# Long-convolution filters read as ready-made Toeplitz blocks instead of being reversed on TensorE

## The reference, cut to what matters

```python
# v = layernorm(x), x1 = x2 = ctx, 8 channels per head, 32 heads h, L = 512
kv = vr[:, :, :, None, :] * x2r[:, :, None, :, :]
y  = irfft(rfft(kv, n=2*L) * rfft(k, n=2*L), n=2*L)[..., :L]   # causal convolution with filter k[h]
y  = y + kv * skip
out = einsum('bhijl,bhil->bhjl', y, x1r)
```

## Time and profile before

| | before |
|---|---|
| median of 3 runs | 3232.25 us (3229.4 to 3232.57) |
| the profiled execution: its time | 3230.03 us |
| its span, first to last instruction | 3228.3 us |
| mean granted TensorE clock | 0.992 of full |
| busy: PE, PEld, DVE, ACT, POOL | 97%, 83%, 67%, 39%, 35% |
| the loop over heads | about 24 to 640 us of the span |
| DMA | 285.83 MB, 89 GB/s in the mean |

### The profile page before, as it was taken

One profiled execution on the slowest core, in us unless ns is written; L12 is line 12 of the kernel. 1 busy time (PEld: TensorE's weight loads), 2 busy tenths in 40 slices (PEclk: granted clock), 3 DMA queues, 4 the chain that ended last, 5 costly groups with the idle time before them and its releaser, 6 DMA issues.

```text
span 3228.3 us, 50126 instructions
## 1 busy us (share of the span) xinstructions
PE 3135.5 (97%) x18517; PEld 2679.9 (83%) x18517; DVE 2167.3 (67%) x5741; ACT 1256.3 (39%) x3041; POOL 1120.6 (35%) x1176
## 2 busy tenths in 40 slices
PE   7999999999999779999999999999999999999999
PEld 4666666689899669999999999999999788888887
DVE  6888888755555568888888888888878533333332
ACT  2333333333344345555555555555555311111111
POOL 7877777625344322222222222222201111011110
PEclk9999999999999899999999999999999999999999
DMA  4544443259777731111111111111100300000000
GB/s 128 153 141 143 132 130 102 77 177 334 226 230 227 246 104 53 47 39 41 47 47 40 41 47 47 47 47 47 47 27 27 108 33 27 27 27 26 27 14 14
DMA packets 129409, 285.83 MB, mean 89 GB/s; under 512 B 18840, under 2 KB 19488, under 8 KB 129168
## 3 DMA queue, kind: packets, MB, share of 16 engines
q1 hardware_dynamic: 100080, 186.49, 18.7%
q0 software_dynamic: 29088, 96.13, 9.1%
HBM read 177.98 MB, written 104.58 MB: 88 GB/s over the span
## 4 chain that ended last, share of the span: by engine, by line
PE 79%; DVE 10%; POOL 7%; DMA 2%; ACT 1%; issue 1%; SPq 0%; POOLq 0%; DVEq 0%
PE g_PH L2444 4%; PE t_U L1727 4%; PE g_O L2460 4%; PE g_PH L2446 4%; PE g_O L2458 4%; PE g_O L2459 4%; PE g_PH L2445 4%; PE t_U L1728 4%; POOL c_kf L1308 4%; PE t_U L1729 4%; PE t_T L1703 3%; DVE c_R L1030 2%; PE t_PO L1713 2%; PE t_PO L1714 2%; DVE c_z L1024 2%; PE t_PO L1715 2%
## 5 line engine op out<-in xcount | busy, mean ns | idle before, releaser
L1857 ACT ACTIVATE t_pr<-t_sm,t_nb 128x256 f32<-128x256 f32 x512 | 256.7, 502 | 368.5 <-DVE t_nb L2067 368.5
L2238 POOL TENSOR_TENSOR t_r<-t_r 128x256 f32<-128x256 f32 x128 | 94.3, 736 | 771.0 <-DVE t_r L2046 425.1
L2516 DVE CAST g_hh<-g_hf 128x512 fp32r<-128x512 f32 x128 | 61.8, 483 | 416.0 <-PE g_O L2460 412.5
L1308 POOL TENSOR_TENSOR c_kf<-c_vt,c_ct 128x512 f32<-128x512 f32 x256 | 298.4, 1181 | 24.8 <-PE f_Y L540 24.8
L2487 ACT ACTIVATE g_hf<-g_PH,b1g 128x512 f32<-128x512 f32 x128 | 88.3, 690 | 502.8 <-PE g_PH L2446 502.8
L2077 DVE TENSOR_SCALAR t_pr<-t_pr,t_rw 128x256 f32<-128x256 f32 x512 | 231.5, 452 | 18.2
L2444 PE MATMUL g_PH<-g_xh,g_w 128*128 128x512 f32 x512 | 203.2, 397 | 6.9 <-DVE g_w L2324 6.9
L545 PE MATMUL f_Y<-c_kh,c_th 128*128 128x512 f32 x448 | 199.8, 446 | 9.1 <-ACT c_kh L776 9.1
L1727 PE MATMUL t_U<-t_voh,t_oth 128*128 128x512 f32 x512 | 202.2, 395 | 0.0
L1728 PE MATMUL t_U<-t_voh,t_otl 128*128 128x512 f32 x512 | 201.6, 394 | 0.0
L2446 PE MATMUL g_PH<-g_xl,g_w 128*128 128x512 f32 x512 | 200.5, 392 | 0.0
(11 more groups left out here) (356 smaller groups left out, 9889.0 us busy)
## 6 DMA issues: line engine op xcount, KB each, us to landing
xs<-c_zero SPq DMA_DIRECT2D x71, 256.0 KB, 5.2
f_xg<-xs SPq DMA_DIRECT2D x71, 256.0 KB, 3.5
ys<-f_yt POOLq DMA_DIRECT2D x71, 256.0 KB
c_tr<-kpad SPq DMA_DIRECT2D x60, 256.0 KB, 4.8
f_xg<-xn SPq DMA_DIRECT2D x40, 256.0 KB
c_xt<-x SPq DMA_DIRECT2D x32, 256.0 KB, 3.5
c_cr<-ctx SPq DMA_DIRECT2D x32, 256.0 KB, 3.9
c_ct<-ctxh SPq DMA_DIRECT2D x32, 256.0 KB, 4.2
```

The lines of the kernel that those rows point to most:

```text
L1308: gp.tensor_tensor(o, iv, ic, ALU.mult).then_inc(*GP("kv", n))
L1857: ac.activation(m.pr[:, N % 2, t, :], m.sm[:, k4, :], ACT.Exp, bias=m.nb[:, k4, 0:1], scale=-1.0, accum_out=m.rw[:, k4, 0:1]).then_inc(*A( ...
```

## The change

The host lays the filters out as the Toeplitz blocks themselves, an f32 array `kt` of 32 x 128 x 512, with rows in their final order. A head's blocks come by one plain DMA into `t`, which has three buffers. ACT copies `t` to `th` (fp32r), and POOL subtracts to get `tl` (128 x 512), where it added 128 x 256 before; for head 0 DVE makes that one subtraction. The plain f32 products read `t` itself. Gone are both reversal products on PE, the copy of `tl` on ACT, `filter_sum`, the matrix `anti`, the split at the start with its trip to DRAM, and the waits that these needed. Tiles that carry no data keep all other tiles where they were.

```diff
-    m.anti = c("anti", [128, 128])[:, :]
-    m.antir = c("antir", [128, 128], F32R)[:, :]
-    m.tr = c("tr", [128, 2, 2, 512], F32R)
+    c("gap", [128, 768])
+    m.t = c("t", [128, 3, 512])
...
-    m.t0 = c("t0", [128, 2, 256])
+    c("gap2", [128, 512])
...
# SP, load(h)
-        if h < 2:
-            sp.dma_start(m.xg[:, s, :], filter_diagonals(d["k"][h, 1:2])).then_inc(*Q[f"t{s}"]("tf", h))
-            return
-        w.wait_ge(*Q["ko"]["kp", 1])
-        w.wait_ge(*PE["pt" if h < 4 else "pt2", h - 2])
-        for q in range(2):
-            sp.dma_start(f32(m.tr[:, s, q, :]), filter_diagonals(d["kpad"][q, h, 1:2])).then_inc(*Q[f"t{s}"]("tf" if q else "tfa", h))
+        w.wait_ge(*PE["y", 8 * (h - 3) + 7])
+        sp.dma_start(m.t[:, h % 3, :], d["kt"][h]).then_inc(*Q[f"t{h % 3}"]("t", h))
...
# PE
-                if u == 1 and lb == 0 and more:
-                    filter_hi(h + 1)
-                if u == 1 and lb == 2 and more:
-                    filter_lo(h + 1)
...
-                w.wait_ge(*GP["t0", h])
                 w.wait_ge(*GP["kv", n])
-                t = pe.matmul(Y, m.t0[:, s, c], m.kf[:, v, mb, :], start=False, stop=mb == lb)
+                t = pe.matmul(Y, m.t[:, h % 3, c], m.kf[:, v, mb, :], start=False, stop=mb == lb)
...
-            w.wait_ge(*(VE if h < 2 else AC)["tl", h])
+            w.wait_ge(*(GP if h else VE)["tl", h])
...
# ACT, filter_hi(h) at u=1, lb=0; filter_lo at u=1, lb=2 is gone
-        w.wait_ge(*PE["pt", h])
+        w.wait_ge(*Q[f"t{h % 3}"]["t", h])
         w.wait_ge(*PE["y", 8 * (h - 2) + 7])
-        copy(m.th[:, s, :], m.PT[:, :]).then_inc(*AC("th", h))
+        copy(m.th[:, s, :], m.t[:, h % 3, :]).then_inc(*AC("th", h))
...
-    w.wait_ge(*Q["kp"]["k"])
-    copy(m.kq[0], m.kr[:, :]).then_inc(*AC("kq"))
...
# DVE: filter_lo for head 0 only; kq[1] and antir are gone
-    w.wait_ge(*AC["kq"])
-    ve.tensor_tensor(m.kq[1], m.kr[:, :], f32(m.kq[0]), ALU.subtract).then_inc(*VE("kq"))
...
# POOL, in the place of filter_sum(h + 1), at u=1, lb=2
-        gp.tensor_tensor(m.t0[:, s, :], f32(m.th[:, s, 0:256]), f32(m.tl[:, s, 0:256]), ALU.add).then_inc(*GP("t0", h))
+        gp.tensor_tensor(m.tl[:, s, :], m.t[:, h % 3, :], f32(m.th[:, s, :]), ALU.subtract).then_inc(*GP("tl", h))
...
-    filter_sum(0)
     residual(0)
     power(1)
-    w.wait_ge(*VE["kq"])
-    for q in range(2):
-        gp.dma_start(d["kpad"][q], f32(m.kq[q])).then_inc(*Q["ko"]("kp", q))
...
+def toeplitz(k):
+    k = np.pad(k, ((0, 0), (128, 0)))
+    return np.ascontiguousarray(np.stack([k[:, 128 - p:640 - p] for p in range(128)], 1))
```

More of the change, by code:

```diff
@@ L124, in c @@
         return sb(nc, low, f"c_{name}", shape, dt)
-    m.anti = c("anti", [128, 128])[:, :]
-    m.antir = c("antir", [128, 128], F32R)[:, :]
-    m.kr = m.xg[0:32, 2:4, :].rearrange("p a b -> p (a b)")[:, 0:640]
-    m.kq = [v[0:32, :, :].rearrange("p a c -> p (a c)")[:, 0:640] for v in (xh0, xl0)]
-    m.tr = c("tr", [128, 2, 2, 512], F32R)
+    c("gap", [128, 768])
+    m.t = c("t", [128, 3, 512])
     m.ones_b = c("ones_b", [128, 128])[:, :]
@@ L339, in turn_at @@
     return None
-def filter_diagonals(ap, partitions=128):
-    return bass.AP(ap.tensor, ap.offset, [[1, partitions], [1, 512]])
 def sync_front(sp, w, K):
@@ L414, in fill @@
         w.wait_ge(*Q[f"n{i % 2}"]["nd", i])
-        w.wait_ge(*PE["pt", 1])
-        w.wait_ge(*Q["ko"]["kp", 1])
         sp.dma_start(m.xg[:, s, :], d["xn"][128 * i:128 * i + 128, :]).then_inc(*Q[f"g{s}"]("in", what))
@@ L426, in sync_front @@
     load(1)
-    sp.dma_start(m.kr[:, :], d["k"]).then_inc(*Q["kp"]("k"))
     for n, (to, of) in enumerate(((m.gw[:, :, :], "gw"), (m.b1s[:, :], "sb1"), (m.rb, "rb1"), (m.ob[:, :, :], "f0b2"))):
@@ L493, in tensor_front @@
     ident = K.ident
[L495 to L510, removed]
     def turn_v(h):
@@ L584, in turn_shared @@
         t.then_inc(*PE("tx", what))
-    filter_hi(0)
-    filter_lo(0)
     turn_v(0)
@@ L619, in hidden @@
             w.wait_ge(*VE["sx", LAST])
-        if n == 1:
-            w.wait_ge(*AC["tl", LAST])
         for kk in range(4):
@@ L843, in shared_rows @@
         w.wait_ge(*PE["tx", row(i)])
[L844 to L847, removed]
+        w.wait_ge(*PE["ph", 4 * (G - 2) + 3])
         copy(m.xhs[G % 2][:, :, 128 * t:128 * t + 128], m.PR[:, :].rearrange("p (k c) -> p k c", k=4)).then_inc(*AC("xh1", i))
@@ L988, in shift, with filter_lo @@
         ve.tensor_scalar(m.nm[:, s, :], m.ag[:, s, 0:1], m.rs[:, s, :], -1.0, ALU.mult, ALU.mult).then_inc(*VE("nm", h))
[L990 to L994, removed]
+    def filter_lo():
+        w.wait_ge(*AC["th", 0])
+        ve.tensor_tensor(m.tl[:, 0, :], m.t[:, 0, :], f32(m.th[:, 0, :]), ALU.subtract).then_inc(*VE("tl", 0))
     def weigh(h):
@@ L1086, in shared_rows @@
         w.wait_ge(*AC["xh1", i])
[L1087 to L1090, removed]
+        w.wait_ge(*PE["ph", 4 * (G - 2) + 3])
         ve.tensor_tensor(lo, m.PR[:, :].rearrange("p (k c) -> p k c", k=4), f32(hi), ALU.subtract).then_inc(*VE("xl1", i))
-    w.wait_ge(*GP["anti"])
-    ve.tensor_copy(m.antir, m.anti).then_inc(*VE("antir"))
     stats(0)
-    filter_lo(0)
+    filter_lo()
     shift(0)
@@ L1282, in power_rows, with filter_lo @@
         gp.tensor_tensor(m.rs0[:, s, :], m.rs0[:, s, :], mhalf, ALU.pow).then_inc(*GP("rs0", i))
-    def filter_sum(h):
+    def filter_lo(h):
         s = h % 2
         w.wait_ge(*AC["th", h])
-        w.wait_ge(*(VE if h < 2 else AC)["tl", h])
-        w.wait_ge(*PE["y", 8 * (h - 2) + 7])
-        gp.tensor_tensor(m.t0[:, s, :], f32(m.th[:, s, 0:256]), f32(m.tl[:, s, 0:256]), ALU.add).then_inc(*GP("t0", h))
+        gp.tensor_tensor(m.tl[:, s, :], m.t[:, h % 3, :], f32(m.th[:, s, :]), ALU.subtract).then_inc(*GP("tl", h))
     def residual(h):
@@ L1326, in gpsimd_front @@
     gp.memset(mhalf, -0.5).then_inc(*GP("mhalf"))
-    gp.memset(m.anti, 0.0).then_inc(*GP("an0"))
-    w.wait_ge(*GP["an0"])
-    gp.affine_select(out=m.anti, in_=m.anti, compare_op=ALU.not_equal, fill=1.0, base=-127, pattern=[[1, 128]], channel_multiplier=1).then_inc(*GP("anti"))
     v3 = m.ones_b.rearrange("p (b j) -> p b j", j=8)
@@ L1365, in gpsimd_front @@
                 if u == 1 and lb == 2 and more:
-                    filter_sum(h + 1)
+                    filter_lo(h + 1)
                 n = (2 * h + u) * 4 + lb + 4
@@ L2546, in layouts @@
     c = np.ascontiguousarray
-    a = {"x": c(i["x"]), "ctx": c(i["ctx_2048"]), "k": c(np.pad(i["L0_xattn_k"], ((0, 0), (128, 0))))}
+    a = {"x": c(i["x"]), "ctx": c(i["ctx_2048"]), "kt": toeplitz(i["L0_xattn_k"])}
     ctx = i["ctx_2048"]
@@ L2581, in layouts @@
     return a
-DMA_COUNTS = ("sk", *(f"x{i}" for i in range(4)), *(f"c{i}" for i in range(3)), "r0", "r1", "t0", "t1", *(f"o{i}" for i in range(4)), "z", "kp", "ko",
+DMA_COUNTS = ("sk", *(f"x{i}" for i in range(4)), *(f"c{i}" for i in range(3)), "r0", "r1", "t0", "t1", "t2", *(f"o{i}" for i in range(4)), "z",
               "cc", "n0", "n1", "w0", "w1", "ti", *(f"g{i}" for i in range(RING)), "q0", "q1", "a0", "a1", *(f"s{i}" for i in range(RING)),
@@ L2591, in program @@
 def program(nc, d):
-    d["kpad"] = nc.dram_tensor("kpad", (2, NHC, 640), F32, kind="Internal").ap()
     for n in ("x1", "xa", "x2", "x3"):
```

## The result

The changed kernel takes 3243.97 us (median of 7 runs, 3239.77 to 3248.59) against 3232.13 us (7 runs, 3229.4 to 3233.63). The ratio is 1.0037 with a 95% interval of 1.0027 to 1.0047: slower by 8.7 to 15.2 us. The forecast was 3243.0. The profiled execution took 3244.61 us with a span of 3242.9 us, 14.6 us more span than before.

What follows compares the result with a forecast made beforehand. The prediction took a ring of waits through DVE, POOL, ACT and PE to bound the kernel. Terms 16.2 - 5.2 - 0.4 = +10.6 us on 3232.25 gave about 3243 us; 8-in-10 range 3228 to 3251, likeliest case 3241 to 3247.

Steps and rivals of the forecast that it cites:

- The ring DVE, POOL, ACT, PE: Loop over heads: a chain of waits through these engines and back to DVE sets the turn, 18.94 us.
- the rival that PE is the bound: Loop: PE's work sets the turn, so removing the reversal products saves 14.4 us; 3212.6 us, chance 0.08.
- POOL's subtraction: In `filter_sum`'s place in the loop: 1.24 us for 0.70, 0.54 a turn over 30 turns, 16.2 us slower.
- The start: Before the loop: earlier first `th` and no POOL wait after its power bring the first product 5.2 us sooner.
- PE's new wait: Before `conv(h+1, 0, 0)`: PE stalls about 1.2 us for `tl`, hidden by 0.2 us before `turn_v`; value 0.
- The rival that this stall comes onto the ring: Before `turn_v`: PE needs 0.3 us more in 22 turns, 6.6 us more; 3249.5 us, chance 0.12.
- The last turn: End of the loop, where PE leads: it saves 0.47 us and waits 0.1 for `tl`, a gain of 0.4.
- The absorbed case: POOL's stretch: if `weigh` moves out, 0.5 of the added 0.54 us a turn comes back; 3227.9 us, chance 0.08.

Runs made afterwards that it cites:

- the first experiment: Changed kernel with POOL's subtraction for `tl(h+1)` moved to u=1, lb=0, ahead of `power_rows`, where POOL waits for DVE; 3216.95 us, ratio 0.9956.

## Why the prediction was right

**The bound.** The ring DVE, POOL, ACT, PE was read rightly. Three runs bear on it: the same subtraction in another place moves the time by 25 to 27 us, a wider sum alone by 16.8 us, and 14.4 us of PE's work by nothing. Two of the readings against the rival that PE is the bound were loose. The 97% is the mean over the span; in the turn of the earlier trace rows it is 98.5%. And the 33.5 us are waits of the weight loads, which run ahead; PE itself waited for those logits for much less, though in each of the 26 turns:

```profile
PE f_PV L519 <- ACT c_lg L776: 12.7, 26, 1.2
```

That PE had some slack was enough here, as the experiments show.

**POOL's subtraction**, forecast at 0.54 us a turn and 16.2 us in all. Measured: from the filter operation in the earlier trace rows at 43.10 to the one at 599.70 before, and from 38.01 to 613.03 after, 29 turns took 18.4 us more, of which 2.9 are the clock's drop; 15.5 / 29 is 0.53 us. With the 30th turn, 16.1 us.

**The start**, forecast at 5.2 us: 5.25 at the first product, 5.1 where the ring begins. The load landed in 5.30 us, inside the bounds.

**PE's new wait**, forecast as hidden with 0.2 us to spare: hidden, but with nothing to spare. PE waited 1.03 us for `tl` in an ordinary turn, where about 1.2 was forecast. PE got to `turn_v` 5.63 us after the end of `c_tl` and not after 5.44: 0.14 us passed from POOL's end to PE's start, and the first product behind the wait took up 0.47. POOL's and ACT's branch took the same 5.63, where the forecast had 5.66. The rival that this stall comes onto the ring was half right: it is on the chain, and costs nothing in an ordinary turn, since the run with the wider sum and without the wait has the same 19.49. That this term came out at 0 is in part luck: the forecast left 0.2 us between the branches, and they turned out to end together.

**The last turn**, forecast as a gain of 0.4: about 0.2 (from the filter operation to `conv` 1.38 us in place of 1.62). The forecast took 1.24 for the 1.38 and left out the same 0.14 us from POOL's end to PE's start.

**Not foreseen.** The wait is longer behind a `choose`, and behind one of the three a drop of the clock cost 2.9 us, in all three profiled executions in which PE's wait for `tl` was left as it is. It is probably a price of the wait, which one run speaks for and none shows. This is most of the 4 us by which the spans differ more (14.6) than the forecast (10.6). The medians, 11.8 and 11.3 us apart on two occasions, lie closer to the forecast.

**The absorbed case** spoke of the lock between DVE's two-input operations and POOL's. The rule of the Trainium skill that stands there (SBUF — State Buffer, the two separate sides: the later operation is blocked until the earlier has ended) held in each of the four places looked at: `weigh` and the residual, `kl` and `tl`, `tl` and the power, and `weigh` with the products. In the first three the one held up ended 0.4 to 1.1 us after the other's end, somewhat less than what it takes alone. What I did not do was to apply it to a place of my own: the first experiment came out 11.5 us above its forecast, and the order that avoids just that collision gave back 9.7.

## What to carry to other kernels

Read one turn of a loop as a ring of waits before counting what an edit adds and takes: here 14 us of matmuls were worth nothing although PE was 97% busy, and 0.54 us a turn on an engine at 78% cost 16 us. An operation that is put on POOL belongs where POOL waits, and there out of the way of DVE operations on SBUF that are on the ring, above all those with two inputs; the place was worth 25 to 27 us and the order within the place another 10. A wait newly given to PE is not sure to be free because a slack covers it: look also at its longest instance and at the granted clock behind it.

## What the runs showed of the hardware that was not expected

- A wait of PE of 1.46 us, with one of 0.71 us 2.1 us before it and four transposes in between, was followed by 1.2 GHz for 6.8 us and cost 2.9 us; the same pair of waits in two other turns of the same kernel was not. With the first wait at 0.25 us the drop came all the same; with the second at 0.55 us, filled by products, it was absent. Single waits of 1.43 us in the run with the subtraction behind `kl` brought none. What singles out the one turn is open.
- The holding-up between DVE and POOL goes both ways, and also strikes small operations: POOL's power, 128 x 1, took 0.93 in place of 0.55 us beside a DVE subtraction of 0.68 us that had begun 0.17 us earlier.
- It is not confined to DVE operations with two inputs: DVE's conversion of 128 x 16 numbers from one tile took 0.89 in place of 0.17 us, from 0.44 us after the start of POOL's subtraction to its end.
